# A small clear on GpSimd behind every indirect scatter of a two-layer decoder

## What is computed

```python
# layer 0
x = x + mamba(layernorm(x))
x = x + cross_attention(layernorm(x), ctx)      # 16 heads of 8, nan guard
x = x + moe(layernorm(x))                       # 8 experts, top 2, gelu, 128 -> 512 -> 128
# layer 1
x = x + self_attention(layernorm(x))
x = x + cross_attention(layernorm(x), ctx)
x = x + moe(layernorm(x))                       # 8 experts, top 2, silu gate, 128 -> 256 -> 128
```

## Time and profile before

| What | us |
|---|---|
| Time, median of 3 runs (1449.87 to 1450.81) | 1450.72 |
| The profiled execution's own time, which is its span | 1552.4 |
| POOL busy in that span | 771.3 (50%) |
| PE busy | 1214.8 (78%) |
| DVE busy | 1011.3 (65%) |
| ACT busy | 902.7 (58%) |

### The profile page before, as it was taken

One profiled execution on the slowest core, in us unless ns is written; L12 is line 12 of the kernel. 1 busy time (PEld: TensorE's weight loads), 2 busy tenths in 40 slices (PEclk: granted clock), 3 DMA queues, 4 the chain that ended last, 5 costly groups with the idle time before them and its releaser, 6 DMA issues. The chain is left out here.

```text
span 1552.4 us, 31341 instructions
## 1 busy us (share of the span) xinstructions
PE 1214.8 (78%) x11210; PEld 936.1 (60%) x11218; DVE 1011.3 (65%) x2376; ACT 902.7 (58%) x1718; POOL 771.3 (50%) x590
## 2 busy tenths in 40 slices
PE   6898989898768887675599938998699886538882
PEld 2666766676564665454499935666356664428772
DVE  5999999999997786555111117886379675433334
ACT  3988898889744886442355527776366453213333
POOL 1999999998954123444355531110113243346552
PEclk8999999999999998766699979999799787659996
DMA  5241222122000311111688732000200001047665
GB/s 191 84 143 55 111 84 84 56 111 84 28 1 8 56 40 31 51 34 55 198 246 257 231 79 55 15 16 16 75 2 25 24 26 35 29 146 208 204 204 174
DMA packets 98028, 138.51 MB, mean 89 GB/s; under 512 B 13965, under 2 KB 77402, under 8 KB 93684
## 3 DMA queue, kind: packets, MB, share of 16 engines
q1 hardware_dynamic: 85764, 117.08, 25.3%
q0 software_dynamic: 9088, 17.07, 3.2%
q10 hardware_dynamic: 3024, 2.36, 0.5%
HBM read 105.91 MB, written 28.19 MB: 86 GB/s over the span
## 5 line engine op out<-in xcount | busy, mean ns | idle before, releaser
L353 POOL TENSOR_TENSOR M_dbx<-M_u,M_b_sb 128x1024 f32<-128x1024 f32 x127 | 296.8, 2364 | 33.2 <-DVE M_e L440 15.5
L454 DVE TENSOR_TENSOR_SCAN M_h<-M_pA,M_dbx 128x512 f32<-128x512 f32 x256 | 298.2, 1207 | 6.5 <-ACT M_pA L612 6.2
L612 ACT ACTIVATE M_pA<-M_dt,M_a_neg 128x504 f32<-128x504 f32 x256 | 175.0, 684 | 21.7 <-DVE M_h L454 17.4
L2159 POOL DMA_INDIRECT F_slots<-F_line,F_pos x128 | 127.1, 993 | 54.4 <-issue 37.9
L2532 PE MATMUL X_bank<-F_xT,F_wbuf 128*128 128x256 f32 x624 | 152.4, 388 | 0.0
L1864 PE MATMUL X_bank<-L_ident,X_s_sb 128*128 128x128 f32 x512 | 94.6, 312 | 69.7 <-ACT X_pt_sb L1727 63.0
L622 ACT ACTIVATE M_hc<-M_pT,M_cT 128x256 f32<-128x256 f32 x256 | 119.8, 469 | 42.9 <-PE M_pT L759 41.5
L1727 ACT ACTIVATE X_pt_sb<-X_bank 128x512 f32<-128x512 f32 x128 | 76.3, 596 | 105.7 <-PE X_bank L1864 105.4
L1552 DVE TENSOR_REDUCE X_smax<-X_bank 128x8 f32<-128x512 f32 x128 | 82.3, 685 | 82.7 <-PE X_bank L1855 80.9
L775 PE MATMUL M_pY<-M_ident,M_hc 128*128 128x128 f32 x1024 | 135.1, 275 | 0.4
L775 PEld LDWEIGHTS M_pY<-M_ident,M_hc 128*128 128x128 f32 x1024 | 125.0, 192 | 0.3
(11 more groups left out here) (339 smaller groups left out, 2810.1 us busy)
## 6 DMA issues: line engine op xcount, KB each, us to landing
M_b_sb<-M_rows_bc SPq DMA_DIRECT2D x32, 1024.0 KB, 4.7
F_wbuf<-in_F_wcat SPq DMA_DIRECT2D x39, 578.0 KB
F_wbuf<-in_F_wcat SPq DMA_DIRECT2D x39, 450.0 KB
X_s_sb<-F_slots SPq DMA_DIRECT2D x39, 132.0 KB
F_xblk<-F_slots SPq DMA_DIRECT2D x39, 132.0 KB
F_line<-F_line SPq DMA_DIRECT2D x16, 256.0 KB
S_ya<-F_answers SPq DMA_DIRECT2D x16, 256.0 KB, 5.7
F_slots<-F_pad ACTq DMA_DIRECT2D x16, 132.0 KB
```

The costliest lines, as they stand in the source:

```text
L353: pool.tensor_tensor(dbx[:, k % DBXS, :, :], u[:, g % 2, :, :], bc(b_sb[:, n, :], 1, 2), ALU.mult).then_inc(dbx_ready, 1)
L454: v.tensor_tensor_scan(h[:, k % STATES, half, :], pA[:, (2 * k + half) % DECAYS, :, :].rearrange("p b t -> p (b t)"), dbx[:, k % DBXS, hal ...
L612: act.activation(pA[:, (2 * k + half) % DECAYS, :, 1:SEQ], dt[:, g % 2, half, :].rearrange("p (b t) -> p b t", t=SEQ)[:, :, 1:SEQ], ACT.Ex ...
L2159: pool.indirect_dma_start(slots, bass.IndirectOffsetOnAxis(pos[:, g, k, t:t + 1], 0), line[:, g % RING, k, t, :], None, bounds_check=E * C ...
```

## The change

Each of the two expert stages' dispatch gets a buffer `space` of 128 x 256 floats (1 KB of each partition) that nobody reads, and a semaphore `spaced`. A function `gap` makes POOL wait until its previous clear of that buffer is done and then clear it again. It is called behind every row scatter and, in the expert stage, behind every pair of answer scatters: 64 + 39 clears in a phase, 206 in the program.

```diff
@@ dispatch_stage
+    space = m.sb("space", [P, 2 * P])
+    spaced = Count(m.sem("spaced"))
@@
+    def gap(pool):
+        reach(pool, spaced.sem, spaced.n)
+        spaced(pool.memset(space[:, :], 0.0))
+
+    st.gap = gap
@@ pool_scatter, in the loop over two scatters
                                     oob_is_err=False).then_inc(scattered[g % RING], 16)
+            gap(pool)
@@ pool_answers, in the loop over blocks, behind the loop over s
+            d.gap(pool)
```

## The result

| | before | after |
|---|---|---|
| First comparison, median us | 1450.30 (4 runs) | 1463.75 (4 runs) |
| Ratio, 95% interval | | 1.0090 [1.0059, 1.0122] |
| Comparison repeated, median us | 1451.04 (23 runs) | 1461.76 (9 runs) |
| Ratio, 95% interval | | 1.0075 [1.0050, 1.0099] |
| Span of a profiled execution | 1446.5 (a second profile) | 1463.5 |

The change costs 10.7 to 13.4 us. The forecast was 1453.9 with a range from 1447 to 1460: the direction was right, the 3.2 us forecast are between a quarter and a third of what came, and the time lies above the range.

The account below looks back on a forecast made before the run. PE, ACT and DVE were taken to pace the attention and weight loads F1, POOL setting the end only at the dispatch and answers' ends. Terms 2.7 + 0.2 + 0.3 = 3.2 us on 1450.7 gave 1453.9, range 1447 to 1460.

Parts of the forecast that it names:

- The cost of one clear, d = 0.20: On POOL between two scatters: starts go from 1.28 to 1.48 us apart, so each clear adds 0.20 us, bounds 0 to 0.34.
- The 0.13 from two clears that start 0.25 us apart: Alternative price of a clear on POOL, from the spacing of starts: 0.13 us each, sum below 2.1 us, not 3.2.
- Group 5's eight clears: Dispatch: 1.6 us of clears hidden under 3.35 us of POOL idle before group 6's scatters; 0.5 charged in X0, nothing in X1.
- POOL paces the last groups: Rival for the dispatch: POOL is the bound from group 5 on, all 17 clears show in each phase, 1458 to 1463; chance 0.15.
- The last seven clears: Dispatch end: seven clears between the last 8 scatters take 1.4 us of POOL; half, 0.7 a phase, reaches SP's row load.
- the floor rival: Rival: clears hide in POOL's 0.30 or pads and weights hold the dispatch's last landing anyway; 0.5 to 1.7 us, 1451.5; chance 0.25.
- The dispatch's two ends: Ends of the dispatch in both phases: 2 x (0.4 + 0.7) + 0.5 = 2.7 us.
- The clears between: Attention, groups 1 to 6: POOL idles 7.6 us or more ahead of the powers, so clears there were counted as nothing.
- The answers, 0.5 us: Answers' end: 0.2 us in F0 and 0.3 in F1; other blocks' clears lie in POOL's idle, 3.3 us per three blocks.
- The 101.7 us: Profiled execution of 1552.4 us against 1450.7 timed: the excess, mostly late PE signals during scatters, was taken to belong to profiling.

Follow-up runs that it names:

- clears_behind_bias: Changed kernel with the eight clears of each of groups 0 to 4 moved behind POOL's bias additions; ratio 1.0037 to the kernel before.
- early_bias_before: Kernel before with the first cross attention's bias additions ahead of a group's first scatter, not behind its sixth; ratio 1.0215 to the kernel before.
- answers_only: Changed kernel without the 128 row clears, keeping the 78 clears behind pairs of answer scatters; ratio 0.9972 to the kernel before.
- after_again: The changed kernel once more, unchanged; ratio 1.0075 to the kernel before.
- rows_only: Changed kernel keeping the 128 clears behind row scatters, without the 78 behind pairs of answers; ratio 1.0058 to the kernel before.
- early_power_after: Changed kernel with an edit meant to move group 7's power earlier that left the instruction order as it was; ratio 1.0100 to the kernel before.
- power_first_after: Changed kernel with group 7's power moved ahead of group 6's first two row scatters; ratio 1.0044 to the kernel before.
- before_again: The kernel before, unchanged, profiled a second time; ratio 0.9981, profiled span 1446.5 us.

## Why the prediction was wrong

- **The cost of one clear, d = 0.20: right.** 0.18 to 0.19 measured, and the two other lengths lie on the same sum (0.97 + the clear + 0.17) within 0.02. The 0.13 from two clears that start 0.25 us apart was too low for a clear behind a scatter.
- **Group 5's eight clears, "in the profile that is enough": the step that failed in the tail.** The 3.35 us of idle belonged to that one execution. Undisturbed, POOL paces groups 5 and 6, and ten clears a phase, not two, stand ahead of the last power: 1.9 us in place of 0.4 in X1. This is the rival "POOL paces the last groups", to which I gave 0.15. That its 1458 to 1463 comes near the measured time is luck: it needed d = 0.34 (by its own formula 12.1, not 12.2), and at the measured d it says 1457 to 1458.
- **The last seven clears, half of 1.4 a phase: mis-sized the other way.** 1.6 of it came back in X1, as in the floor rival. The dispatch's two ends cost 2.3 + 1.9 = 4.2 us, where I had 2.7 and the rival 6.8. The edits bear this out with some scatter: with the clears of groups 5 to 7 alone the two stretches P6-A take 55.3 and 51.8 us, with those of groups 0 to 4 alone 53.4 and 50.8, before 52.1 and 50.5.
- **The clears between, "POOL idles 7.6 us or more": the step that failed in the attention.** I took idle time of an engine as room. It isn't when what ends it is a chain that starts at the same engine. Six clears put the bias additions 1.2 us later, and the holds on DVE with them; `clears_behind_bias` takes that away and `early_bias_before` shows how large it can be. I had not looked for operations whose duration depends on POOL. In after it is 0.8 to 1.2 us in each group of X0 that runs at full clock and none in one with 10 us at 1.2 GHz (25.9 us in both kernels), 1.4 net from P1 to P6. In X1 it is nothing that can be told. So this step failed in kind, but it is a small part of the error. The premise itself was read from the long execution: undisturbed, POOL idles 4.5 to 5.9 us ahead of the powers of groups 2 to 4 and 6 in X1.
- **The answers, 0.5 us: not refuted**, but on a cover that was 0.29 us a block and not 1.1: `answers_only` loses nothing that can be told.
- **The 101.7 us: right that the timed medians have none of it; its cause stays open.** That it belongs to profiling is not borne out, as every other profile is without it. The right use would have been not to take a single bound from that execution's idle times, as I did three times.
- **The clock: put at nothing without a reason, and the largest term of the traces.** 3.4 us in self attention and 5.9 in X1 of after's trace are PE at 1.2 GHz. Four traces of kernels with all the row clears and their order (`after`, `after_again`, `rows_only`, `early_power_after`) have both; `power_first_after` has neither the one nor the long drop in X1. In the timed runs, where before too meets some of this, about 3.4 of 10.1 us go with the clock.

The account of after's trace is thus: dispatch ends 4.2, holds in X0 1.4, clock 9.3, answers' stage 1.1 (the traces of one and the same F1 differ by more), start 0.7. The first two, 5.6, are shown by edits that take them away or move them, and the 6.7 +- 1.0 that the timed runs show at an equal clock agree with them. That the rest is the clock is read from traces and runs; no experiment switched it. Why the changed kernel nearly always meets the late rise, whether by where its stages start or by how PE is loaded ahead of them, stays open.

## What to carry to other kernels

Idle time of an engine is room only if what ends it does not start at that engine: follow the chain behind the wait back until it leaves the engine, and if it doesn't, every instruction ahead of its start counts in full. Before adding to GpSimd's queue, look for VectorE operations whose duration varies, and see with what on GpSimd they end; moving the work that holds them, not shortening it, was worth 0.45% here and a wrong place cost 2%, each time with some of the clock in it. A few us between two kernels, or between two traces, mean little until their granted clocks are compared. And before a profile's idle times are used as bounds, its span must agree with the timed runs; a second profile of the same kernel is the cheapest experiment there is.

## What the runs showed of the hardware

- Indirect scatters start 1.28 us apart without a clear between them and 1.28, 1.46 and 1.68 us apart with clears of 0.12, 0.33 and 0.55: the shortest is free, the others cost their duration less 0.15.
- A 0.16 us VectorE operation lasted 1.95 us (and 1.96 in a later group) while GpSimd ran a scatter's end, a clear and an addition. Having begun during the scatter, it did not end between the three, but with the last.
- Two GpSimd additions a group, moved onto VectorE's row normalisation, cost 29 us by the medians with no instruction added, 12.5 at an equal clock.
- The granted clock came back to 2.4 GHz 5 us (`before_again`, `power_first_after`) or 14 us (after, `rows_only`) after PE's first work of the same stage, at starts that differed by 4.8 us or by only 0.3.
- The same attention stretch with the same instructions took 108.0 us at a mean granted clock of 1.00 and 114.8 at 0.93.
